# Gate and up matmuls of two row pairs merged into one with 256 moving columns

## What is computed

```python
x = x + tanh(g_xattn[0]) * xattn(layernorm(x), ctx, ctx)
x = x + tanh(g_ffn[0])   * ffn(layernorm(x), W_gate, W_up, W_down)

# xattn: per batch and head the circular correlation of q and k over 64 positions (by FFT), the 8 best
# lags of each channel, a softmax over them, and the sum of v shifted by these lags (index clamped)
# ffn:
gate = einsum('bsh,mh->bsm', x, W_gate)
up   = einsum('bsh,mh->bsm', x, W_up)
out  = einsum('bsm,hm->bsh', silu(gate) * up, W_down)
```

## Time and profile before

| | |
|---|---|
| three runs | 213.7, 213.95, 213.95 us; median 213.95 |
| profiled execution | span 212.1 us from its first to its last instruction; the page gives no other time for it |
| PE | busy 203.6 us, 2700 matmuls, granted clock full throughout |
| DVE, ACT, POOL | busy 135.7, 131.4, 122.4 us |
| DMA | 17.9 MB, most of it in the first 40 us |

### The profile page before, as it was taken

One profiled execution on the slowest core, in us unless ns is written; L12 is line 12 of the kernel. 1 busy time (PEld: TensorE's weight loads), 2 busy tenths in 40 slices (PEclk: granted clock), 3 DMA queues, 4 the chain that ended last, 5 costly groups with the idle time before them and its releaser, 6 DMA issues.

```text
span 212.1 us, 6601 instructions
## 1 busy us (share of the span) xinstructions
PE 203.6 (96%) x2700; PEld 147.8 (70%) x2700; DVE 135.7 (64%) x408; ACT 131.4 (62%) x207; POOL 122.4 (58%) x151
## 2 busy tenths in 40 slices
PE   7889799999999999999999999999999999999993
PEld 2344369855398866795689665896598669859992
DVE  2499978977987884689478933898454426412411
ACT  2581776789897989697947894986335713502220
POOL 1200658588598977589848596797724734610430
PEclk9999999999999999999999999999999999999999
DMA  6999986420222201002011211120213300211001
GB/s 154 338 416 434 389 297 137 106 44 12 49 35 47 25 3 38 14 3 51 0 28 30 49 28 25 53 53 2 71 31 66 134 3 0 77 25 53 5 0 51
DMA packets 20734, 17.89 MB, mean 84 GB/s; under 512 B 16096, under 2 KB 16992, under 8 KB 20320
## 3 DMA queue, kind: packets, MB, share of 16 engines
q1 hardware_dynamic: 20704, 17.47, 27.5%
HBM read 10.65 MB, written 2.10 MB: 60 GB/s over the span
## 4 chain that ended last, share of the span: by engine, by line
PE 89%; DVE 5%; ACT 1%; DMA 1%; issue 1%; POOL 1%; DVEq 0%; POOLq 0%
PE psum L937 48%; PE psum L1121 23%; PE psum L920 6%; PE psum L1071 3%; PE psum L928 2%; PE psum L1056 2%; DMA x_sb<-x 1%; PE psum L1048 1%; PE psum L1014 1%; DVE top L792 1%; DVE probs L814 1%; DVE raw_stats L759 1%; PE psum L1016 1%; PE psum L1015 1%; DVE prod L782 1%
## 5 line engine op out<-in xcount | busy, mean ns | idle before, releaser
L937 PE MATMUL psum<-xt_hi,wu 128*128 128x128 f16 (+1 forms) x504 | 54.0, 213 | 0.0
L937 PE MATMUL psum<-xt_lo,wu 128*128 128x128 f16 (+1 forms) x504 | 54.0, 213 | 0.0
L937 PE MATMUL psum<-xt_hi,wg 128*128 128x128 f16 (+1 forms) x504 | 54.0, 213 | 0.0
L937 PE MATMUL psum<-xt_lo,wg 128*128 128x128 f16 (+1 forms) x504 | 53.9, 213 | 0.0
L632 POOL TENSOR_TENSOR hid_lo<-hid,hid_hi 128x512 f16<-128x512 f32 (+2 forms) x32 | 33.6, 1055 | 28.8 <-ACT hid_hi L750 28.7
L937 PEld LDWEIGHTS psum<-xt_hi,wg 128*128 128x128 f16 x504 | 44.8, 98 | 5.6 <-issue 5.0
L937 PEld LDWEIGHTS psum<-xt_hi,wu 128*128 128x128 f16 x504 | 45.0, 98 | 3.2 <-issue 2.4
L937 PEld LDWEIGHTS psum<-xt_lo,wu 128*128 128x128 f16 x504 | 45.1, 98 | 0.7
L937 PEld LDWEIGHTS psum<-xt_lo,wg 128*128 128x128 f16 x504 | 45.0, 98 | 0.6
L1121 PE MATMUL psum<-wd,hid_hi 128*128 128x512 f16 (+1 forms) x126 | 43.3, 356 | 0.0
L1121 PE MATMUL psum<-wd,hid_lo 128*128 128x512 f16 (+1 forms) x126 | 43.3, 355 | 0.0
(11 more groups left out here) (95 smaller groups left out, 340.9 us busy)
## 6 DMA issues: line engine op xcount, KB each, us to landing
wg<-w_gate SPq DMA_DIRECT2D x1, 1792.0 KB, 8.9
wu<-w_up SPq DMA_DIRECT2D x1, 1792.0 KB, 12.8
wd<-w_down SPq DMA_DIRECT2D x1, 1792.0 KB, 16.9
out<-x_sb SPq DMA_DIRECT2D x7, 256.0 KB, 2.3
x_sb<-x SPq DMA_DIRECT2D x4, 256.0 KB, 4.8
ctx_sb<-ctx SPq DMA_DIRECT2D x4, 256.0 KB, 4.8
ctx_sb<-ctx SPq DMA_DIRECT2D x1, 1024.0 KB, 18.6
x_sb<-x SPq DMA_DIRECT2D x1, 1024.0 KB, 20.6
```

The costliest lines, as they stand in the source:

```text
L937: last = nc.tensor.matmul(psum[:, bank, a * n:(a + 1) * n], w[:, k, m * P:(m + 1) * P], xt[:, e, k, tok], start=(k == 0 and part == 0), st ...
```

## The change

Pairs 2+3, 4+5 and 6+7 form groups. Their gate and up matmuls take both pairs as moving operand: 2 x 128 rows from two neighbouring slots of xt_hi and xt_lo, which now have four slots (`p % 4`). A step has two blocks of 128 hidden columns, so its result again fills one PSUM bank (2 blocks x 2 pairs x 128), and a group has 7 steps (`gate:2` to `gate:2.6`, named by the group's first pair). tanh, silu, hid, h_hi and h_lo follow these steps with 512 elements each. `down` stays per pair and follows when hidden values are there; its two results lie in the two banks of one slot. The first gate of a group waits for the rows of both pairs. w_whole, a buffer used for pair 0 alone, now lies in v_turned, with a wait for its last reader. ORDER is new for all engines. The second half of the last store is issued by ACT, the last step of the program. Pairs 0 and 1 keep their steps.

```diff
-STEPS = 4
+GROUPS = ((0,), (1,), (2, 3), (4, 5), (6, 7))
+def ffn_steps(p):
+    return len(SPANS) if len(group_of(p)) == 1 else MT // 2
-    w_whole = sb("w_whole", [P, 2, D])
+    w_whole = v_turned[:, 0, :, :]
-    xt_hi = sb("xt_hi", [P, 2, KT, P], f16)
+    xt_hi = sb("xt_hi", [P, 4, KT, P], f16)
     def ffn_step(p, s):
+        if len(group_of(p)) == 2:
+            return (2 * s, 2 * s + 2), slice(0, P)
...
                 if step == "store":
-                    for h, cols in enumerate(halves(p)):
-                        sp.wait_ge(out_ready, p + h + 1)
-                        sp.dma_start(outv[:, p:p + 1, cols], x_sb[:, p:p + 1, cols]).then_inc(stored, 16)
+                    cols = halves(p)[0]
+                    sp.wait_ge(out_ready, p + 1)
+                    sp.dma_start(outv[:, p:p + 1, cols], x_sb[:, p:p + 1, cols]).then_inc(stored, 16)
...
+                if step == "store_half":
+                    act.wait_ge(out_ready, PAIRS + 1)
+                    nc.scalar.dma_start(outv[:, p:p + 1, halves(p)[1]], x_sb[:, p:p + 1, halves(p)[1]])\
+                      .then_inc(half_stored, 16)
...
-            def widen(w, bank, e, span, tok):
-                n = tok.stop - tok.start
+            def widen(w, bank, p, span, tok):
+                group = group_of(p)
+                n = len(group) * (tok.stop - tok.start)
                 for a, m in enumerate(range(*span)):
+                    o = psum[:, bank, a * n:(a + 1) * n]
+                    if len(group) == 2:
+                        o = o.rearrange("p (e t) -> p e t", e=2)
                     for k in range(KT):
                         for part, xt in enumerate((xt_hi, xt_lo)):
-                            last = nc.tensor.matmul(psum[:, bank, a * n:(a + 1) * n], w[:, k, m * P:(m + 1) * P],
-                                                    xt[:, e, k, tok], start=(k == 0 and part == 0),
+                            moving = xt[:, p % 4, k, tok] if len(group) == 1 else xt[:, p % 4:p % 4 + 2, k, :]
+                            last = nc.tensor.matmul(o, w[:, k, m * P:(m + 1) * P], moving,
+                                                    start=(k == 0 and part == 0),
                                                     stop=(k == KT - 1 and part == 1))
...
                         if n == 0:
-                            for part in range(2):
-                                pe.wait_ge(x_moved[part][e], nth_moved(p))
-                            pe.wait_ge(hid_done, STEPS * p)
+                            for q in group_of(p):
+                                for part in range(2):
+                                    pe.wait_ge(x_moved[part][q % 2], nth_moved(q))
+                            pe.wait_ge(hid_done, first_step(p))
```

235 lines of the change are left out of this document (134 added, 101 removed).

## The result

The changed kernel takes 217.68 us (median of 216.33, 217.27, 218.09 and 218.53) beside 213.95 for the kernel before: ratio 1.0168, 95% interval 1.0132 to 1.0205. It is slower by 3.7 us; the prediction was 212.5. The profiled execution spans 216.1 us where it was 212.1. The medians in this document leave out the few executions that ran slow as a whole (from 217.5 us in i1 to 349.7 in the kernel before). First the page: busy shares, clock, the chain that ended last by engine.

The account below looks back on a forecast made before the run. PE, already at its column rate without gaps from 28 us on, was taken to bound the kernel. -1.75 - 0.15 + 0.5 + 0 = -1.4 us gave a 210.7 us span and 212.5 us, range 211.8 to 213.9.

Parts of the forecast that it names:

- The merge: Gate and up of pairs 2 to 7: 672 matmuls of 256 columns pay the fixed part half as often, -1.75 us.
- the change doesn't do what it says: Rival in merged gate and up: two runs cost the fixed part twice, giving 214.25 us; chance 0.04.
- the weight load sets the pace: Rival in gate and up: halving the weight loads would save 37.5 us, giving about 176 us; chance 0.01.
- The Trainium skill's spacing: Gate and up: 81 ns at 128 columns, 131 at 512, would save 43 us; the prediction let the trace decide against it.
- The order after that: Queues after the front: some PE waits end late at tight steps, +0.5 us in all, between 0 and 2.5.
- the model: Pair 5's path from mix to landed transpose, 8.6 us, taken for pair 7's before gate:6, covered by 9.5 us.
- The front: Up to 25 us, where DVE sets the pace: its new order fills waits, -0.15 us, between -0.3 and +0.3.
- The tail: Last out and stores: later out +0.25, store from ACT's queue -0.3 at one end, +0.4 at the other; taken as 0.
- this rival: PE before gate:6 waits for x_t:7.1, losing 2.6 us in place of 0.5, giving 214.6 us; chance 0.09.
- Spread stalls eat the gain: Rival after the front: stalls of 1.5 to 2.3 us at tight steps, giving 213.5 to 214.3 us; chance 0.13.

Follow-up runs that it names:

- i1: Merged kernel with the front of the kernel before and all later queues laid out anew, wspec:3 behind up:1 and kspec:5 behind up:1.2 on PE: 214.96 us.
- g2: g1 with each merged gate and up matmul split into two of 128 columns: 218.31 us.
- g1: Changed kernel with the front of the kernel before up to kspec:3, then all five queues laid out anew, mixes cut into parts: 216.53 us.
- j2: j1 with each merged gate and up matmul split into two of 128 columns: 215.20 us.
- j1: Merged kernel, front of the kernel before, queues laid out anew, lags:3 ahead of down:0, sub8 and mask kept from starting inside POOL instructions: 213.35 us, ratio 0.9954.
- e2: Changed kernel with only SP's order edited, transpose x_t:2 issued ahead of x_t:2.1: 217.27 us.
- e4: Changed kernel with three edits for pair 7: exp:7 ahead of tanh:4.3, mask:7 behind total:7, store:2 behind w_t:7.1: 217.14 us.
- g3: Changed kernel with the front of the kernel before, up to kspec:3, for all engines: 218.10 us.
- g4: Kernel before with one SP step, turn:1.3, moved early to right behind vcopy:1: 215.07 us, ratio 1.0041.

## Why the prediction was wrong

**The merge: right.** -1.75 us was predicted from a pace that is a straight line through three widths, and the two runs of 128 cost no second fixed part: 109.1 ns. With the order held fixed the merge gives 1.78 (g2 less g1) and 1.85 us (j2 less j1). That "the change doesn't do what it says" and that the weight load sets the pace have both fallen. The Trainium skill's spacing ("TensorE: Matmul & The Clock Gate", section "Back-to-back issue gap"), by which the prediction estimated 43 us, is not borne out: 1.75 us came.

**The order after that: the step that failed.** The prediction laid the queues beside PE at kspec:5, lags:5, gate:2 and mix:5, found each within 0.3 us, and said "I take 0.5 us in all". They are 4.1: 3.42 in the three late gaps and 0.65 in stretched steps. The failure has three parts.

First, the wrong places were looked at. Of the late steps only lags:5 was among the tight ones, and it was taken to be 0.1 late where it is 1.06. wspec:3 and wspec:7 were not looked at at all; the 92% for ACT was a mean over 68 us, and no mean tells what stands at the head of a line, such as k_lo:5 on POOL or exp:7 on ACT. Second, the comparison used a step's own engine and left out SP's queue: x_t:2.1 ahead of x_t:2, and store:2 between the transposes of pair 7, are to be read in the order (e2 and e4 show their price). Third, durations were taken as constants. A transpose was 2.5 us, at most 3.4; at wspec:3 it took 4.1, with a program block in the way. The mask at wspec:7 took 1.23 us with POOL running, and sub8 1.22 instead of 0.23 (i1 and j1). Those can't be read off an order: they depend on what runs at the same moment. But the trace of the kernel before had them. The 3.4 is the longest of tile xt_lo's seven; xt_hi's reached 4.2, and pair 5, which was the model, is an unhindered case. sub8 and the mask stand there at 1.18 and 1.66 us too. First xt_hi's transposes, then DVE at 99 us, both in the kernel before:

```profile
DMA to landing us min/median/max: 2.4/2.5/4.2
```

```profile
99.09 1.18 DVE L802 TENSOR_TENSOR expo<-top 128x64 f32<-128x64 f32 x1
```

The old order had room for them. "A stall at one gives room to the next, so they don't add up in full" was wrong as well. Five gaps of 0.4 to 1.2 us stood one after the other. There is truth in it only for time won early (g3).

**The front: the second step that failed.** The term of -0.15 looked at DVE, and gate:0 did start 0.40 us earlier. But SP works in the front too, and turn:1.3, moved 13 us ahead into full queues, makes PE halt for 1.65 us; put into the kernel before it costs 1.28 (g4). The front's term is +1.25 in place of -0.15 (gate:0.2 at 38.55 instead of 37.30). The step that failed is that only DVE was looked at there, and not what SP issues. In this order the term was hidden behind the late steps (g3), so it is not simply added to the 4.1.

**The tail: right within 0.1.** 0 was predicted; the last landing comes 3.8 us after PE's end, 3.65 before. ACT issues the last half at 213.3 within 0.37 us.

**The rivals.** gate:6 is not late: 44 down matmuls in 9.51 us and then gate:6. The change was slower, as this rival ended, but by another mechanism. "Spread stalls eat the gain" is what happened, at nearly twice the price it was given: 4.1 us, and the front's 1.65, where at most 2.3 stood. Its chance of 0.13 rested on "the old order ran 180 us without a gap"; that an order was laid out well once says nothing for another one.

**Open.** Of j1 against before 0.6 us are won where the merge alone is worth 1.75 to 1.85. One fetch of a program block and 0.34 us explain most of the rest in the profiled execution, but in the shorter ones nothing was profiled. I did not find an order that keeps all of the gain, and no run shows whether there is one. Whether the late fetch near 34 us in the changed kernel comes from the copies' bytes or from their pieces was not tried. Why a fetch holds up a transpose is not shown either, only that the two go together.

## What to carry to other kernels

A matmul merge that saves 1.75 us is real but small beside what a new order of five queues can lose: hold the order fixed when you price the one, and for the other walk every chain that ends in a PE step, with SP's and POOL's queues in it, not only the four that look tight. Moving PE's steps alone, or mending one gap, moves the stall; lay out all queues together. Keep attention matmuls in whole blocks, keep copies out of the time of the big loads, and plan each step that waits for a transpose with its longest landing (4.4 us here), not the median.
